# A decoder layer on one core: the set-up of its expert feed-forward stage in another order

## The chip, the cores and the metric

The kernel runs on one core of one Trainium2 chip. The core has five engines that run side by side and meet at semaphores: PE (TensorE, matrix products), ACT (ScalarE), DVE (VectorE), POOL (GpSimd) and SP (SyncE), which here issues all DMAs. The metric is the time of one execution in microseconds (us), lower is better.

## What is computed

One decoder layer over 16 batches of 100 tokens with 128 features: self-attention, cross-attention of 16 heads against a context of 1444 rows, and a feed-forward part with 1024 experts chosen by product keys, each followed by a layer norm. The change touches the third part. Cut to what matters:

```
q = einsum('bnd,de->bne', x, w_q)                    # 2048 = 2 * 8 heads * 128
mean, var = q.mean((0, 1)), q.var((0, 1))            # over all 1600 tokens
q = (q - mean) * rsqrt(var + 1e-5) * bn_gamma + bn_beta
sim = einsum('pbnhd,hkpd->pbnhk', q, keys)           # 32 keys for each of 16 (side, head)
sx, ix = top_k(sim[0], 8); sy, iy = top_k(sim[1], 8)
scores, pk = top_k(all 64 sums of sx and sy, 8)      # -> 8 experts per head
h = gelu_new(x . down_embed[indices]) * softmax(scores)
out = sum of h * up_embed[indices]
x = layernorm(x + out)
```

The kernel never makes q. With cov the 128x128 covariance of the tokens, the variance of column e of q is w_e' cov w_e. So it makes cov, then the 16 variances' groups, scales the keys with gamma / sqrt(var), and folds w_q and the keys into one 128x512 matrix `sim_w`. The similarities of a token are (x - mean) times `sim_w`, plus a constant row `sim_c` = beta times keys.

## The kernel before

`decoder` runs three functions one after the other: `front` (self-attention), `cross`, `ffn`. At the end of each all engines meet, so no engine begins `ffn` before the last batch's `x2` is done. `x2` ([100, 16, 128], tokens of a batch on the partitions) is the output of `cross` and the input of `ffn`. Inside a function each engine has its own list of instructions, written out by hand in the order in which it runs them; an engine waits where its next instruction waits, and everything behind it in the list waits too.

**cross.** 16 batches of 13 tiles (slots 0 to 12 of a batch; 208 tiles). POOL's list goes slot by slot: low halves of the probabilities in slots 0, 3, 4 and 7 (L811), low halves of the queries (`q_lo`, L800), the power for the context's norm in slot 8 (`crs`, L565), the norm itself in slots 9 to 11 (`xh`, L576), and more. A batch's `x2` is finished by DVE (L965) in slot 5 of the next batch.

**ffn, set-up.** SP issues eight loads (L1170), all on one semaphore: `f_wq` (1 MB), `f_wqt` (w_q transposed, two halves of 0.5 MB), `f_keys` (0.25 MB), `f_gam`, `f_bet` (8 KB each), `f_down`, `f_up` (0.5 MB each). PE turns the 16 batches of `x2` (L1500, four groups of four batches) and ACT copies them to `x2T`, adding up each row as it goes (L1219); DVE makes the mean from these sums (L1299, L1301) and centres the four groups into `xcT` (L1305). PE then waits for all eight loads, makes the constant row (16 small products, L1504), turns `xcT` back (L1512; ACT copies to `xct`, L1226), and makes the covariance (16 products over the batches, L1517; ACT: `cov`, L1228). Next the 16 products of `f_wq` with `cov` (L1521), four to a PSUM bank. DVE multiplies each bank by `f_wqt` (L1319) and sums (L1322), corrects the 16 variances twice (L1325, L1327), POOL takes the power -1/2 (`vrs`, L1189), DVE makes `gain` and `kscaled` (L1329, L1331), PE folds (16 products of `f_wqt` with `kscaled`, L1526), ACT copies to `sim_w` (L1238).

Beside this run two other chains. The constant row is split into three bf16 parts: ACT takes the high part (L1223), DVE the rests (`c_rest`, `c_part`, L1308 to L1314), ACT writes them into `sim_c` (L1235, L1236). And three tables of numbers for the one-hot comparisons, `iota_w` (128x128x128), `iota_c` and `iota_j`, are spread out by ACT (L1230 to L1232).

**ffn, steps.** Seven steps of 256 tokens (two halves `hf` of 128; the last has 64 tokens). A step: similarities (PE, L1537 and L1538), their copy `simb` (ACT, L1245), on DVE the 8 largest of each of 32 rows of keys (L1383) and their indices (L1394), then the best pairs, the softmax, and the one-hot tables `oneh`, `eqc`, `mv_hi`, `mv_lo` (L1471 to L1481). From these PE gathers the weights of the experts, 512 products of 16 columns a step (L1560, L1561). PE also makes the experts' hidden values (L1546) and ACT their gelu (L1252). ACT's `idxw` (L1259) and the exponential `esc` (L1283) are needed by DVE in the middle of the step; gelu and exponential need different activation tables, so ACT loads a table before each (ACT_TABLE_LOAD). Gathering of a step runs beside DVE's work of the next.

Of the kernel before, what the change touches and what calls it, by code (L numbers as in the profile page):

```python
# [9 lines left out]
ALU = mybir.AluOpType  # L10
# [3 lines left out]
P = 128  # L14
# [669 lines left out]
def cross(nc, a, m, ps):  # L684
# [6 lines left out]
    with ExitStack() as ctx:  # L691
# [28 lines left out]
        pad_done, cur_done = sem("pad_done"), sem("cur_done")  # L720
# [65 lines left out]
        def _(pool):  # L786
# [32 lines left out]
            current(0)  # L819
            for k in range(P_BUF):  # L820
# [250 lines left out]
def ffn(nc, a, m, ps, out):  # L1071
# [4 lines left out]
    with ExitStack() as ctx, ExitStack() as early:  # L1076
# [6 lines left out]
        ident, nhalf, x2 = m["ident"], m["nhalf"], m["x2"]  # L1083
# [37 lines left out]
        xct = sb("xct", [S, B, D], until=early)  # L1121
        msum, mean = sb("msum", [D, NG], until=early), sb("mean", [D, 1], until=early)
# [8 lines left out]
        f_ld, f_waited = sem("f_ld"), sem("f_waited")  # L1131
        fc_done, x2T_ps, x2T_done, mean_done, xcT_done = (sem(n) for n in ("fc_done", "x2T_ps", "x2T_done", "mean_done", "xcT_done"))
        xct_ps, xct_done, cov_ps, cov_done = (sem(n) for n in ("xct_ps", "xct_done", "cov_ps", "cov_done"))
        cw_ps, cw_done, var_done, vrs_done, gain_done = (sem(n) for n in ("cw_ps", "cw_done", "var_done", "vrs_done", "gain_done"))
        simc_ps, simc_hi, simc_rest, simc_done = (sem(n) for n in ("simc_ps", "simc_hi", "simc_rest", "simc_done"))
        simw_ps, simw_done, wide_done = sem("simw_ps"), sem("simw_done"), sem("wide_done")
# [7 lines left out]
        block = ctx.enter_context(nc.Block())  # L1144

# [15 lines left out]
        def _(sp):  # L1161
            for dst, src in ((f_wq[:, :], a["L0_ffn_w_q"]),
                             (f_wqt[:, 0:FH, :], a["ffn_wq_t"][0:FH * KD, :].rearrange("(n e) d -> e n d", e=KD)),
                             (f_wqt[:, FH:NB, :], a["ffn_wq_t"][FH * KD:NB * KD, :].rearrange("(n e) d -> e n d", e=KD)),
                             (f_keys[:, :, :], a["ffn_keys_t"].rearrange("e s h k -> e (s h) k")),
                             (f_gam[:, :], a["L0_ffn_bn_gamma"]),
                             (f_bet[:, :], a["L0_ffn_bn_beta"]),
                             (f_down[:, :], a["ffn_down_t"]),
                             (f_up[:, :, :], a["L0_ffn_up_embed"].rearrange("(c e) d -> e c d", e=P))):
                sp.dma_start(dst, src).then_inc(f_ld, 16)  # L1170
# [8 lines left out]
        def _(pool):  # L1179
            pool.iota(iota_i[:, :], pattern=[[1, P]], base=0, channel_multiplier=0).then_inc(fc_done, 1)  # L1180
# [7 lines left out]
            pool.wait_ge(var_done, 3)  # L1188
            pool.tensor_tensor(out=vrs[:, :], in0=var[:, :], in1=nhalf[:, 0:NB], op=ALU.pow).then_inc(vrs_done, 1)  # L1189
# [26 lines left out]
        def _(act):  # L1216
            for k in range(NG):
                act.wait_ge(x2T_ps, k + 1)
                act.activation(x2T[:, k * G * S:(k + 1) * G * S], ps[:, k, 0:G * S], ACT.Copy,  # L1219
                               accum_out=msum[:, k:k + 1]).then_inc(x2T_done, 1)  # L1220
            act.wait_ge(fc_done, 6)
            act.wait_ge(simc_ps, 1)
            act.activation(sim_c[0:1, :], ps[0:1, 6, :], ACT.Copy).then_inc(simc_hi, 1)  # L1223
            for k in range(NG):
                act.wait_ge(xct_ps, k + 1)
# [441 lines left out]
```

## Time and profile before

| | |
|---|---|
| time, median of 3 runs | 1341.62 us (1341.55 to 1344.81) |
| profiled execution | 1341.98 us, of which the span 1340.2 us |
| PE busy | 1156.0 us, 86% |
| DVE busy | 1152.7 us, 86% |
| ACT busy | 876.6 us, 65% |
| POOL busy | 620.2 us, 46% |

The span goes from the first to the last instruction of the profile. Busy shares are means over stages that differ: `cross` takes some 910 us, the set-up of `ffn` some 45 us, its steps some 267 us. PEclk in the rows below is the clock granted to TensorE as a share of its full speed; it has two levels, 0.50 (1.2 GHz) and 1.00 (2.4 GHz), and a value between them is a mean over a stretch that holds both.

### The profile page before, as it was taken

The numbers are of one execution on the slowest core, as the hardware profiler recorded it, in microseconds if no ns is written. First come the engines' busy times: TensorE is split into PE (matmuls) and PEld (weight loads), VectorE is DVE, ScalarE is ACT, GpSimd is POOL, SyncE is SP. The second block draws the span as 40 slices with busy tenths as digits, with TensorE's granted clock in tenths as the row PEclk, the third lists the DMA queues.
The fourth block names the chain that finished last, engine by engine and source line by source line (L and its number), as shares of the span: only waits on it lengthen the run. The fifth ranks groups of instructions, "written<-read, shape, count | busy, mean of one in ns | idle before, by whom it ended". The sixth has DMA issues, their size and how long they took to land. (4 is left out here: it accounts for less than half of the span.)

```text
span 1340.2 us, 32623 instructions
## 1 busy us (share of the span) xinstructions
PE 1156.0 (86%) x12753; PEld 900.3 (67%) x12758; DVE 1152.7 (86%) x2860; ACT 876.6 (65%) x1202; POOL 620.2 (46%) x512
## 2 busy tenths in 40 slices
PE   3576999999999999999999999999995639777778
PEld 2463677777777767776777777777674628677668
DVE  5796899999999999999999999998884288999984
ACT  0246888889888888888888888888872632222121
POOL 2344667566675667757577575775220000000000
PEclk9768999999999999999999999999997766666666
DMA  7007999999999999999999999999997000000000
GB/s 156 1 6 139 191 191 187 203 200 190 200 192 201 193 194 196 199 198 198 193 200 198 195 199 193 184 184 173 189 193 162 11 0 2 5 5 6 5 5 6
DMA packets 671121, 185.78 MB, mean 139 GB/s; under 512 B 655828, under 2 KB 668536, under 8 KB 670840
## 3 DMA queue, kind: packets, MB, share of 16 engines
q1 hardware_dynamic: 670968, 183.71, 80.3%
q8 instruction: 100, 1.64, 0.5%
q14 instruction: 53, 0.43, 0.1%
HBM read 19.51 MB, written 0.82 MB: 15 GB/s over the span
## 5 line engine op out<-in xcount | busy, mean ns | idle before, releaser
L1046 PE MATMUL ps<-pT,xa_hi 128*128 128x128 f16 x2288 | 381.1, 217 | 17.5 <-DMA pT<-p 16.7
L851 ACT ACTIVATE e<-ps,bias 128x1444 f32<-128x1444 f32 (+1 forms) x208 | 305.7, 1470 | 132.6 <-DVE bias L923 132.0
L1042 PE MATMUL ps<-pT,xa_hi 128*128 128x128 f16 x2288 | 382.8, 217 | 8.5 <-ACT uT L874 8.2
L1043 PE MATMUL ps<-pT,xa_lo 128*128 128x128 f16 x2288 | 382.8, 217 | 0.0
L921 DVE TENSOR_REDUCE nmax<-ps 128x1 f32<-128x1444 f32 (+1 forms) x208 | 343.9, 1653 | 19.3 <-PE ps L1026 18.6
L933 DVE TENSOR_TENSOR p<-e,p 128x1408 f16<-128x1408 f32 (+3 forms) x288 | 303.9, 1096 | 35.6 <-ACT p L859 34.5
L859 ACT ACTIVATE p<-e 128x1408 f16<-128x1408 f32 (+1 forms) x208 | 288.2, 1386 | 13.3
L811 POOL TENSOR_TENSOR p<-e,p 128x1408 f16<-128x1408 f32 (+1 forms) x128 | 196.6, 1556 | 182.9 <-ACT p L859 182.9
L1042 PEld LDWEIGHTS ps<-pT,xa_hi 128*128 128x128 f16 x2288 | 222.1, 98 | 33.6 <-issue 19.1
L1046 PEld LDWEIGHTS ps<-pT,xa_hi 128*128 128x128 f16 x2288 | 222.0, 98 | 24.2 <-DMA pT<-p 24.0
L1024 PE MATMUL ps<-xT_hi,q_hi 128*128 128x512 f16 (+1 forms) x624 | 229.9, 368 | 8.0 <-DMA xT_lo<-xa_lo 7.4
L1043 PEld LDWEIGHTS ps<-pT,xa_lo 128*128 128x128 f16 x2288 | 222.0, 98 | 13.7
L1025 PE MATMUL ps<-xT_hi,q_lo 128*128 128x512 f16 (+1 forms) x624 | 229.7, 368 | 0.0
L1026 PE MATMUL ps<-xT_lo,q_hi 128*128 128x512 f16 (+1 forms) x624 | 229.7, 368 | 0.0
L576 POOL TENSOR_SCALAR xh<-raw,cmv,crs 128x127 f32<-128x127 f32 x168 | 185.7, 1116 | 0.0
L800 POOL TENSOR_TENSOR q_lo<-q,q_hi 128x400 f16<-128x400 f32 x64 | 89.4, 1397 | 151.9 <-ACT q_hi L893 151.9
L1560 PE MATMUL ps<-mv_hi,oneh 128*128 128x16 f16 (+1 forms) x832 | 109.2, 214 | 46.0 <-DVE mv_lo L1481 46.0
L1560 PEld LDWEIGHTS ps<-mv_hi,oneh 128*128 128x128 f16 (+1 forms) x832 | 108.7, 174 | 48.9 <-DVE mv_lo L1481 48.4
L1197 POOL TENSOR_TENSOR comb<-top 128x512 f32<-128x512 f32 (+1 forms) x13 | 13.7, 1070 | 220.1 <-DVE top L1383 220.1
L1561 PEld LDWEIGHTS ps<-mv_lo,oneh 128*128 128x128 f16 (+1 forms) x832 | 108.5, 174 | 0.9 <-issue 0.8
L1561 PE MATMUL ps<-mv_lo,oneh 128*128 128x16 f16 (+1 forms) x832 | 109.0, 214 | 0.0
L1026 PEld LDWEIGHTS ps<-xT_lo,q_hi 128*128 128x128 f16 x624 | 61.2, 98 | 66.6 <-issue 1.5
(225 smaller groups left out, 1910.4 us busy)
## 6 DMA issues: line engine op xcount, KB each, us to landing
raw<-in_ctx SPq DMA_DIRECT2D x16, 704.0 KB
pT<-p SPq DMA_TRANSPOSE x416, 4.2
f_wq<-in_L_ffn_w_q SPq DMA_DIRECT2D x1, 1024.0 KB, 4.9
f_wqt<-in_ffn_wq_t SPq DMA_DIRECT2D x2, 512.0 KB, 7.0
raw<-in_ctx SPq DMA_DIRECT2D x48, 18.0 KB
x_tok<-in_x SPq DMA_DIRECT2D x1, 800.0 KB
out_x<-ost SPq DMA_DIRECT2D x6, 128.0 KB, 2.0
wk_t<-in_wk_t SPq DMA_DIRECT2D x1, 512.0 KB, 5.7
```

Source lines behind the costliest of these rows:

```text
L851: act.activation(e32[t % E_BUF][rows, :], score_banks(t)[rows, 0:T], ACT.Exp, bias=bias[rows, t % N_BUF:t % N_BUF + 1]).then_inc(e_done, 1)
L859: act.activation(p[t % P_BUF][rows, 0:TF * P], e32[t % E_BUF][rows, 0:TF * P], ACT.Copy).then_inc(hi_done, 1)
L921: dve.tensor_reduce(nmax[rows, k:k + 1], score_banks(t)[rows, 0:T], AX_X, ALU.max, negate=True).then_inc(max_done, 1)
L933: ins = dve.tensor_tensor(out=p[t % P_BUF][rows, out:out + keys.stop - keys.start], in0=e32[t % E_BUF][rows, keys], in1=p[t % P_BUF][rows, ...
L1024: pe.matmul(out, hi, xT_hi[b % 2][:, keys], start=True, stop=False)
L1025: pe.matmul(out, lo, xT_hi[b % 2][:, keys], start=False, stop=False)
L1026: last = pe.matmul(out, hi, xT_lo[b % 2][:, keys], start=False, stop=True)
L1042: pe.matmul(out, hi, ph, start=n == 0, stop=False)
L1043: pe.matmul(out, lo, ph, start=False, stop=False)
L1046: pe.matmul(out, hi, pl, start=False, stop=False)
L1560: pe.matmul(dst, oneh[0:j, :, s], mv_hi[0:j, 0:nb, s], start=True, stop=False)
L1561: last = pe.matmul(dst, oneh[0:j, :, s], mv_lo[0:j, 0:nb, s], start=False, stop=True)
```

## The change

1. **Mean.** POOL adds up `x2` over the batches during `cross` (new tile `x2sum`, one add in slot 7 of each batch). In `ffn` DVE adds the last batch (`total`), and PE multiplies by a tile of ones: the mean's sum stands once as a row on all partitions and once as a column.
2. **Centring in place.** DVE subtracts the mean from `x2` with its tokens on the partitions (`xc`), four groups; the covariance is made from `xc`. The turns back of `xcT` and the copies `xct` are gone, and so are ACT's row sums.
3. **Order of the turned copies.** Of `x2T` and `xcT` only the first group of 400 tokens is made before the covariance. The other three come after the similarities of step 0 (PE, ACT) and after the indices of step 0 (DVE).
4. **Halves.** Variance corrections (two instructions joined into one), power, `gain`, `kscaled`, folding, `sim_w` and the similarities of step 0 are done for 8 of the 16 (side, head) pairs at a time. Step 0's similarities go to four half-filled banks, and DVE takes its maxima half by half.
5. **Loads.** Order `f_wq`, `f_bet`, `f_gam`, `f_keys`, `f_wqt` (two), `f_down`, `f_up`, with four semaphores instead of one, each waited for where it is used.
6. **Constant's rests** on DVE: behind the first half of the keys, ahead of the last variance sum. The constant row on PE: behind the weight products.
7. **Tables.** `iota_w` in four quarters: POOL one in the set-up, ACT one behind `cov`, ACT one ahead of the first gelu, POOL one behind the first `comb`. `iota_c` and `iota_j` on POOL.

The core of the diff:

```diff
@@ cross, POOL
+                if i == 7 and 0 < b < B:
+                    pool.wait_ge(y_norm, 4 * b)
+                    pool.wait_ge(x2sum_done, b)
+                    pool.tensor_tensor(out=m["x2sum"][:, :], in0=m["x2sum"][:, :], in1=x2[:, b - 1, :], op=ALU.add).then_inc(x2sum_done, 1)
@@ ffn, POOL
             pool.tensor_copy(iota_f[:, :], iota_i[:, :]).then_inc(fc_done, 1)
-            pool.wait_ge(var_done, 3)
-            pool.tensor_tensor(out=vrs[:, :], in0=var[:, :], in1=nhalf[:, 0:NB], op=ALU.pow).then_inc(vrs_done, 1)
+            wide_rows(0)
+            for p in range(2):
+                pool.wait_ge(var_done, p + 1)
+                pool.tensor_tensor(out=vrs[:, key_half(p)], in0=var[:, key_half(p)], in1=nhalf[:, 0:FH], op=ALU.pow).then_inc(vrs_done, 1)
...
             for i in range(NSTEP):
                 combine(i)
+                if i == 0:
+                    wide_rows(1)
@@ ffn, ACT
+            turned_out(0)
+            act.wait_ge(cov_ps, 1)
+            act.activation(cov[:, :], ps[:, 0, 0:D], ACT.Copy, scale=1.0 / NT).then_inc(cov_done, 1)
...
+            weights_out(0)
...
+            first_out(0)
+            weights_out(1)
+            first_out(1)
+            for k in range(1, NG):
+                turned_out(k)
+            wide_rows(3)
@@ ffn, DVE
+            dve.tensor_tensor(out=total[:, :], in0=x2sum[:, :], in1=x2[:, B - 1, :], op=ALU.add).then_inc(total_done, 1)
+            dve.wait_ge(mean_ps, 1)
+            for k in range(NG):
+                ks = slice(k * G, (k + 1) * G)
+                dve.scalar_tensor_tensor(out=xc[:, ks, :], in0=ps[0:S, 3, 0:D].rearrange("s (a d) -> s a d", a=1).to_broadcast([S, G, D]),
+                                         scalar=-1.0 / NT, in1=x2[:, ks, :], op0=ALU.mult, op1=ALU.add).then_inc(xc_done, 1)
...
+                if i == 0:
+                    for k in range(1, NG):
+                        centred(k)
+                    dve.wait_ge(narrow_done, 1)
@@ ffn, PE
+            pe.matmul(ps[0:S, 3, 0:D], ones_s[:, :], total[:, :], start=True, stop=True)
+            pe.matmul(ps[:, 3, D:D + 1], total[:, :], ones_s[:, 0:1], start=True, stop=True).then_inc(mean_ps, 1)
+            turn(0)
+            for b in range(B):
+                if b % G == 0:
+                    pe.wait_ge(xc_done, b // G + 1)
+                last = pe.matmul(ps[:, 0, 0:D], xc[:, b, :], xc[:, b, :], start=b == 0, stop=b == B - 1)
+            last.then_inc(cov_ps, 1)
...
+            sim_weights(0)
+            pe.wait_ge(simc_done, 1)
+            pe.wait_ge(xcT_done, 1)
+            first_sims(0)
+            sim_weights(1)
+            first_sims(1)
+            for k in range(1, NG):
+                turn(k)
```

PE's list from its start in `ffn` (`ps` is PSUM; `ident` stands for a turn). Before:

```order
L1500 MATMUL ps<-ident,x 128x100 x16
L1504 MATMUL ps<-f_keys,f_bet 1x32 x16
L1512 MATMUL ps<-ident,xcT 100x128 x16
L1517 MATMUL ps<-xct 128x128 x16
L1521 MATMUL ps<-cov,f_wq 128x128 x16
L1526 MATMUL ps<-kscaled,f_wqt 128x32 x16
L1537 MATMUL ps<-sim_c,ones_b 128x512
```

And now, up to the other three groups' turns:

```order
L1605 MATMUL ps<-total,ones_s 100x128
L1606 MATMUL ps<-ones_s,total 128x1
L1587 MATMUL ps<-ident,x 128x100 x4
L1611 MATMUL ps<-xc 128x128 x16
L1617 MATMUL ps<-cov,f_wq 128x128 x16
L1622 MATMUL ps<-f_keys,f_bet 1x32 x16
L1593 MATMUL ps<-kscaled,f_wqt 128x32 x8
L1599 MATMUL ps<-sim_c,ones_b 128x256
L1600 MATMUL ps<-sim_w,xcT 128x256
L1599 MATMUL ps<-sim_c,ones_b 128x256
L1600 MATMUL ps<-sim_w,xcT 128x256
L1593 MATMUL ps<-kscaled,f_wqt 128x32 x8
```

The covariance (L1611) has moved ahead of everything that a load is needed for, the constant row (L1622) behind the weight products (L1617), the folding and the first similarities come in two halves.

DVE's list between the weight products and the first maxima. Before:

```order
L1319 TENSOR_TENSOR cw<-ps,f_wqt 128x512
L1322 TENSOR_REDUCE var<-cw 128x4
L1319 TENSOR_TENSOR cw<-ps,f_wqt 128x512
L1322 TENSOR_REDUCE var<-cw 128x4
L1325 TENSOR_SCALAR var<-var 128x16
L1327 TENSOR_SCALAR var<-var 128x16
L1329 TENSOR_TENSOR gain<-vrs,f_gam 128x16
L1331 TENSOR_TENSOR kscaled<-f_keys,gain 128x512
```

And now:

```order
L1362 TENSOR_TENSOR cw<-ps,f_wqt 128x512
L1368 TENSOR_REDUCE var<-cw 128x4
L1362 TENSOR_TENSOR cw<-ps,f_wqt 128x512
L1378 TENSOR_TENSOR gain<-vrs,f_gam 128x8
L1380 TENSOR_TENSOR kscaled<-f_keys,gain 128x256
L1393 TENSOR_TENSOR c_rest<-ps,sim_c 1x512
L1395 CAST c_part<-c_rest 1x512
L1397 TENSOR_TENSOR c_rest<-c_rest,c_part 1x512
L1399 CAST c_part<-c_rest 1x512
L1368 TENSOR_REDUCE var<-cw 128x4
L1372 TENSOR_SCALAR var<-var 128x8
L1378 TENSOR_TENSOR gain<-vrs,f_gam 128x8
```

The keys' first half is scaled ahead of the last variance sum, and the four instructions of the constant's rests stand between the two halves.

ACT's list from the copy of `sim_w` to `esc` of step 0. Before:

```order
L1238 ACTIVATE sim_w<-ps 128x512
L1245 ACTIVATE simb<-ps 128x1024
L1252 ACT_TABLE_LOAD
L1252 ACTIVATE gel<-ps 128x1024 x2
L1259 ACTIVATE idxw<-idxf 128x2048
L1283 ACT_TABLE_LOAD
L1283 ACTIVATE esc<-dsc 128x128
```

And now:

```order
L1275 ACTIVATE sim_w<-ps 128x256
L1279 ACTIVATE sim_c<-c_part 1x512
L1280 ACTIVATE sim_c<-c_part 1x512
L1270 ACTIVATE simb<-ps 128x2x256
L1275 ACTIVATE sim_w<-ps 128x256
L1270 ACTIVATE simb<-ps 128x2x256
L1254 ACTIVATE x2T<-ps 128x400 x3
L1261 ACTIVATE iota_w<-iota_f 128x4096
L1299 ACT_TABLE_LOAD
L1299 ACTIVATE gel<-ps 128x1024 x2
L1306 ACTIVATE idxw<-idxf 128x2048
L1329 ACT_TABLE_LOAD
```

Three turned groups and a quarter of `iota_w` have come between the similarities' copy and the first gelu, with `idxw` and `esc` behind them.

## Rows read from the trace of the kernel before

**Rows 1.** Busy times by stage: us, busy by engine (instructions), PEclk, DMA.

```profile
100.00:1010.00 910.00, 865.97 (x10070) 646.52 (x10071) 829.98 (x1492) 761.87 (x1019) 562.03 (x435) 0.99 1.14 192
1028.00:1073.00 45.00, 26.64 (x168) 23.23 (x169) 10.38 (x22) 23.35 (x21) 4.20 (x7) 0.66 0.26 76
...
1108.00:1340.00 232.00, 188.61 (x2027) 170.53 (x2031) 197.16 (x990) 49.42 (x70) 16.32 (x18) 0.65 0.02 5
```

**Rows 2.** Chain of waits, set-up: start us, us, what, count of records.

```profile
1034.47 6.08 DMA f_up<-in_L_ffn_up_embed
...
1045.73 3.59 PE ps L1517 x32
...
1049.67 1.17 PE ps L1521 x8
...
1056.74 2.94 POOL vrs L1189
...
1060.65 7.05 PE ps L1526 x32
...
1068.85 1.91 PE ps L1538 x2
...
1072.77 1.03 ACT simb L1245
...
1073.92 3.08 DVE top L1383 x32
```

**Rows 3.** Busy times in three stretches with PE at work: PEclk is what counts.

```profile
1040.60:1045.00 4.40, 4.40 (x44) 3.83 (x44) 1.76 (x3) 1.78 (x3) 0.00 (x0) 0.50 0.00 0
1045.20:1053.50 8.30, 7.93 (x69) 7.56 (x68) 2.83 (x5) 5.24 (x4) 0.00 (x0) 1.00 0.01 2
1060.70:1067.70 7.00, 6.99 (x32) 6.85 (x32) 0.00 (x0) 5.86 (x5) 0.00 (x0) 0.50 0.00 0
```

**Rows 4.** Lines in the set-up: engine, shapes, count, busy us, mean ns, idle before.

```profile
L1230 ACT ACTIVATE iota_w<-iota_f 128x16384 f16<-128x16384 f32 x1 | 13.8, 13847 | 0.0
...
L1305 DVE TENSOR_SCALAR xcT<-x2T,mean 128x400 f32<-128x400 f32 x4 | 1.4, 424 | 0.0
...
L1308 DVE TENSOR_TENSOR c_rest<-ps,sim_c 1x512 f32<-1x512 f32 x1 | 0.7, 678 | 9.6 <-ACT sim_c L1223 9.6
```

**Rows 5.** The page's DMA issues: size of each, median us to landing.

```profile
f_wqt<-in_ffn_wq_t SPq DMA_DIRECT2D x2, 512.0 KB, 7.0
```

**Rows 6.** POOL by line over the whole span.

```profile
L576 POOL TENSOR_SCALAR xh<-raw,cmv,crs 128x127 f32<-128x127 f32 x154 | 174.5, 1143 | 0.0
...
L565 POOL TENSOR_TENSOR crs<-cve,nhalf 128x12 f32<-128x12 f32 x16 | 36.4, 2275 | 0.1
...
L791 POOL COPY sc_cur<-sc 128x16 f32<-128x16 f32 x16 | 3.1, 192 | 5.5 <-POOLq L40 5.5
...
L1187 POOL CAST iota_f<-iota_i 128x128 f32<-128x128 int32 x1 | 0.3, 291 | 0.1
```

**Rows 7.** Chain of waits in step 0, as rows 2.

```profile
1077.14 5.26 DVE idx L1394 x33
...
1088.73 0.29 DVE pijf L1428
...
1095.69 8.69 DVE oneh L1471
```

**Rows 8.** Timeline, step 0, ACT: start us, us, engine, instruction [idle before].

```profile
1082.74 1.91 ACT L1259 ACTIVATE idxw<-idxf 128x2048 f16<-128x2048 f16 x1 [3.51 <-DVE idxf L1401]
1084.67 1.28 ACT L1283 ACT_TABLE_LOAD   x1
1085.96 0.31 ACT L1283 ACTIVATE esc<-dsc 128x128 f32<-128x128 f32 x1
```

**Rows 9.** Timeline of PE in the same stretch.

```profile
1095.13 3.62 PE L1546 MATMUL ps<-x2T,f_down 128*128 128x256 f32 x8
```

**Rows 10.** Timeline of POOL behind `crs`, slot 9 of a late batch.

```profile
892.09 1.81 POOL L800 TENSOR_TENSOR q_lo<-q,q_hi 128x400 f16<-128x400 f32 x1 [3.82 <-ACT q_hi L893]
```

More of the change, by code:

```diff
@@ L819, in _ @@
             current(0)
+            pool.memset(m["x2sum"][:, :], 0.0).then_inc(x2sum_done, 1)
             for k in range(P_BUF):
@@ L1144, in ffn, with sim_half, key_half, group @@
         block = ctx.enter_context(nc.Block())
+        HALF_SIM = NB * KEYS // 2
+        def sim_half(p):
+            return slice(p * HALF_SIM, (p + 1) * HALF_SIM)
+        def key_half(p):
+            return slice(p * FH, (p + 1) * FH)
+        def group(k):
+            return slice(k * G * S, (k + 1) * G * S)
         def cols(i):
@@ new lines, in centred, with weighted_cov @@
+            def centred(k):
+                dve.wait_ge(x2T_done, k + 1)
+                dve.tensor_scalar(xcT[:, group(k)], x2T[:, group(k)], mean[:, 0:1], None, ALU.subtract).then_inc(xcT_done, 1)
+            def weighted_cov(k):
+                ns = slice(4 * k, 4 * k + 4)
+                dve.wait_ge(cw_ps, k + 1)
+                if k == 0:
+                    dve.wait_ge(wqt_ld, 32)
+                dve.tensor_tensor(out=cw[:, ns, :], in0=ps[:, k, :].rearrange("e (n d) -> e n d", n=4),
+                                  in1=f_wqt[:, ns, :], op=ALU.mult).then_inc(cw_done, 1)
@@ new lines, in variance, with safe_variance, scaled_keys @@
+            def variance(k):
+                ns = slice(4 * k, 4 * k + 4)
+                dve.wait_ge(cw_done, k + 1)
+                dve.tensor_reduce(var[:, ns], cw[:, ns, :], AX_X, ALU.add).then_inc(sum_done, 1)
+            def safe_variance(p):
+                dve.wait_ge(sum_done, 2 * p + 2)
+                dve.tensor_scalar(var[:, key_half(p)], var[:, key_half(p)], 0.0, EPS, ALU.max, ALU.add).then_inc(var_done, 1)
+            def scaled_keys(p):
+                ns = key_half(p)
+                dve.wait_ge(vrs_done, p + 1)
+                dve.wait_ge(keys_ld, 48)
+                dve.tensor_tensor(out=gain[:, ns], in0=vrs[:, ns], in1=f_gam[:, ns], op=ALU.mult).then_inc(gain_done, 1)
+                dve.wait_ge(gain_done, p + 1)
+                dve.tensor_tensor(out=kscaled[:, ns, :], in0=f_keys[:, ns, :],
+                                  in1=gain[:, ns].rearrange("e (n a) -> e n a", a=1).to_broadcast([KD, FH, KEYS]), op=ALU.mult).then_inc(kscaled_done, 1)
@@ L1307, in _ @@
+            centred(0)
+            for k in range(2):
+                weighted_cov(k)
+                variance(k)
+            safe_variance(0)
+            weighted_cov(2)
+            variance(2)
+            weighted_cov(3)
+            scaled_keys(0)
             dve.wait_ge(simc_hi, 1)
@@ L1314, in _ @@
             dve.tensor_copy(c_part[:, 1, :], c_rest[:, 1, :]).then_inc(simc_rest, 1)
[L1316 to L1333 removed]
+            variance(3)
+            safe_variance(1)
+            scaled_keys(1)
             def weigh(i, n):
@@ L1375, in step @@
                 j, na, nb = nh * HK, nh * NB, nh * NC
-                dve.wait_ge(sim_done, i + 1)
                 if i:
+                    dve.wait_ge(sim_done, i)
                     dve.wait_ge(comb_done, i)
                     dve.wait_ge(pick, 7 * i)
-                dve.sem_inc(f_waited, 1)
+                    dve.sem_inc(f_waited, 1)
+                else:
+                    for p in range(2):
+                        dve.wait_ge(first_done, p + 1)
+                        dve.sem_inc(f_waited, 1)
+                        for hf in range(nh):
+                            for n in range(p * FH, (p + 1) * FH):
+                                ins = dve.max(top[0:w, hf, n, :], simb[0:w, hf, n, :])
+                    ins.then_inc(top_done, 1)
                 for hf in range(nh):
-                    for n in range(NB):
-                        ins = dve.max(top[0:w, hf, n, :], simb[0:w, hf, n, :])
-                    if hf == nh - 1:
+                    if i:
+                        for n in range(NB):
+                            ins = dve.max(top[0:w, hf, n, :], simb[0:w, hf, n, :])
+                    if i and hf == nh - 1:
                         ins.then_inc(top_done, 1)
```

177 lines of the change are left out of this document (85 added, 92 removed).

## The prediction

> **What bounds the kernel now.** I read the stretches by stage first [rows 1]. From 100 to 1010 us PE and DVE are both busy over 90% of the time: that is the cross-attention stage, into which the change puts one short POOL instruction per batch. The set-up of the feed-forward stage (1028 to 1073 us) is different: in 45 us PE is busy 26.6, ACT 23.4 and DVE 10.4 us, so no engine is the bound; it is a chain, one engine working while the others wait. So what counts there is the chain of waits [rows 2]: the last load lands at 1040.55, then turns, 16 covariance products to 1049.3, its copy, four pieces of the variance, POOL's power, the 16 products that fold keys into weights (7.05 us), the first similarities, their copy, and 32 maxima until 1077.0. From there to the first `oneh` at 1095.69 step 0 is DVE's own chain, with hardly a gap [rows 7]. From 1095.69 on the code is the same in both kernels, so the gain is how much earlier `oneh` of step 0 starts, plus or minus what TensorE's clock does to the later steps.
>
> **The sum, from 1028.1 us.** Set-up loads no longer stand ahead of the covariance. New order: DVE adds `x2sum` and the last batch (0.3), PE makes the mean by two fp32 products of full weights (0.44 each at half clock, as 7.05 us for 16 in [rows 2]), so the mean stands at 1029.4. The first `xc` group reads 512 columns from PSUM, as `c_rest` does in 0.68 [rows 4]: 1030.1. Later groups take 0.65 each, less than PE's four products. The 16 covariance products cost 0.22 each at full clock (3.59 us for 16 in [rows 2]) and 0.44 at half. Before, PE took up work at 1040.6, stood at clock 0.50 up to 1045.0 and at 1.00 from 1045.2 [rows 3]. I let it rise as late here, 4.5 us into the products: ten at 0.44 and six at 0.22, done at 1036.1, copied at 1036.4. Before that copy was done at 1049.65 (start of its reader, 1049.67, in [rows 2]). **Saved: 13.2**, with ends 15.5 (all at full clock) and 12.1 (all at half).
>
> The products with the queries' weights then need `f_wqt` too. Its halves landed 7.0 us after issue behind 2 MB [rows 5]; now 0.25 MB of keys and the two small loads go ahead, an eighth more bytes, so 7.9 us: about 1036.9. The first four products are done at 1036.4 + 1.2 = 1037.6, so this load is hidden by only 0.7 us.
>
> DVE runs product, sum, product, sum at 0.7 each (512 columns, as `c_rest` in [rows 4]) and one short correction: 1040.6. POOL's power over 16 columns took 2.94 [rows 2], over 12 it took 2.28 [rows 6], so 0.165 a column and 1.6 for 8: 1042.3. DVE meanwhile does three more pieces (to 1042.6), then gain and half of the keys: 1043.2. PE folds eight keys (1.8 at full, 3.5 at half clock), ACT copies 0.4: 1045.5 to 1047.2. Beside it DVE makes the constant's rests (two of 0.68, two casts of 0.4): 1045.4; ACT writes them, two of 0.6: 1046.8. I take 1046.8, since the rests decide unless the clock has fallen already.
>
> From here the clock matters. All that PE has after 1040.5 are products of 32 columns. Such a run stood at 0.50 for 7.0 us while PE was busy 6.99 of them [rows 3], though 7.9 busy us out of 8.3 had been at 1.00 shortly before. So I take half clock from 1046.8. First similarities at half width: 512 columns took 1.91 [rows 2], so 0.95 for 256 and 0.15 for the bf16 constant, two tokens' halves: 2.2, to 1049.0; ACT 0.6. The second half's scaled keys are ready by 1048.7 (sum 0.7, correction 0.2, POOL 1.7, DVE 0.6 from 1045.4), so PE goes on: eight folds 3.5, ACT 0.4, products 2.2, ACT 0.6: 1055.9. DVE has done half the maxima by 1051.3; the other 16 take 1.54 (3.08 for 32): **maxima done at 1057.5 instead of 1077.0, 19.5 earlier.**
>
> **What comes back.** Two things stand in step 0 that did not. DVE centres the other three groups ahead of `idxf`: four took 1.44 us, so **1.1** for three [rows 4]. And ACT, which before had 3.51 us of idle ahead of `idxw` [rows 8], gets late. From 1055.9 it takes three turned groups (0.8 on PE and 0.5 on ACT each, one PSUM bank for all three, so in turns): 1059.7. Then a quarter of `iota_w`: 13.85/4 = 3.5 [rows 4], 1063.2. Then the table load 1.28 and the first `gel`, 128x1024 from PSUM like `simb`'s 1.03 [rows 2]: 1065.5. PE's second eight `f_down` records take 3.62 at half clock [rows 9]: 1069.2; `gel` 1070.3; `idxw` 1.91: 1072.2; load and `esc` 1.6: 1073.8. DVE gets through 32 indices (5.3, [rows 7]), the three centred groups and `idxf` at 1064.3, and 6.3 us later (1082.71 to 1089.02, [rows 7]) wants `esc`, at 1070.6. It **waits 3.3** (1.6 if PE is at full clock there). Sum: 19.5 - 1.1 - 3.3 = **15.1 us**.
>
> Of the table load the rows show this: it ends at 1085.95 and `esc` starts at 1085.96 [rows 8]. The Trainium skill, page "ScalarE: Activation LUTs", section "What ACT_TABLE_LOAD costs", says that a drain of about 1.38 us comes on top of each load of 1.28. By that rule ACT would be 2.8 us later and the kernel would take 1329.3 us; the row shows no such drain, so that has a chance of 2 in 100.
>
> **Edits costed at nothing.** POOL's new add per batch (100x128) stands behind `low_half` of slot 7 and ahead of `crs`; behind it in the queue are `crs` and `q_lo`. By POOL's rate for two inputs it takes some 0.4 us. POOL then sits idle 3.82 us until `q_hi` comes [rows 10]: covered. Without that cover, 15 times 0.4 is 6 us. Its wait is for the layer norm of the batch before, done many slots earlier. POOL's table pieces: a cast of 128 elements takes 0.29, a power over one column more costs 0.165 [rows 6]; the copy of 16 columns takes 0.19, so 0.86 ns an element: `iota_c`, `iota_j` and a quarter of `iota_w` (6208 elements) are done by 1035.5, and POOL is wanted at 1040.6. At the worst rate that a cast allows (0.29 for 128, 2.27 ns) they end at 1044.3, 3.7 late. ACT's first quarter fits between 1036.4 and the constant at 1042. POOL's second quarter starts at 1059.7 and is wanted at 1080.6.
>
> **Rivals.** (1) The clock holds. If PE stays at 1.00 after 1045, folds take 1.8 and products 1.2: second copy at 1053.0, maxima at 1054.5 (22.5 earlier), ACT late by only 1.3; 20.1 us saved, **1321.5**. For it: once up, it held through 8.3 us [rows 3]. Against: the narrow products above. 20 in 100. (2) The clock rises late, or a load or POOL is. With all products at half clock the copy is at 1037.5, the 16 weight products end at 1044.6, the constant row at 1046.5, its rests are written at 1050.6 instead of 1046.8: 3.8 lost, 11.3 saved, **1330.3**. `f_wqt` 3 us late or POOL at 2.27 ns give about the same. For it: only 0.7 us of cover on the load, and PE idles before 1028. 20 in 100. (3) The gain is given back in later steps: they run at a mean clock of 0.65, PE 188.6 of 232 us [rows 1], and the stretches at full clock may fall elsewhere. The three runs already lie 3.3 us apart. To take back 11 us or more PE would have to lose 6% of its time there with DVE never covering: 3 in 100, about **1339**. (4) Slower: POOL's pieces ahead of the power. The one-input `xh` instruction costs 1.14 us for 127 elements, 9 ns each [rows 6]. At that rate 6208 elements end at 1086, 45 us after the variance, and the second quarter 16 us after `oneh` wants it: 61 - 15 = 46 us slower, **1388**. It decides from 4.9 ns an element on. Against: `xh` has two per-partition operands, the cast row has none. 2 in 100.
>
> **Numbers.** The profiled run took 1341.98 us (span 1340.2), 0.36 above the median of 1341.62. 1341.62 - 15.1 = 1326.5. The forecast holds 53 in 100, beside the 2 of the drain. Rivals 1 and 2 give 1321.5 and 1330.3; with some 2 us either way for the later steps' clock the range is 1319.5 to 1332.5. A measurement tells 0.3%, 4 us, from no change: faster 0.95, same 0.03, slower 0.02.
>
> **What the profile after should show.** The copy of `cov` ends 8.3 us after the stage starts (21.6 before); PE's first fp32 products of 32 columns start at once behind the weight products, with no wait for DMA; maxima of step 0 done 29.4 us in (48.9 before); DVE waits some 3 us for `esc` in step 0; `oneh` starts 52.5 us in (67.6 before). The forecast is wrong if PE waits for `f_wqt` or `f_wq`, if POOL still copies when the variance is ready, if the clock in the second half of the set-up is 1.00, or if the stretch from `oneh` to the end is not 244.5 us within 3.

## The result and the profile after

| | before | after |
|---|---|---|
| time, median | 1342.78 us (1341.55 to 1344.81, 4 runs) | 1325.98 us (1325.4 to 1329.02, 4 runs) |
| ratio, with its 95% interval | | 0.9878 (0.9857 to 0.9899) |
| profiled execution, its span | 1341.98, 1340.2 us | 1325.4, 1323.7 us |

The changed kernel is 16.8 us faster by the medians. The forecast was 1326.5 with a range from 1319.5 to 1332.5. Six further runs in a group of their own gave the same ratio, 0.9878 (`c_after` below).

The page of the changed kernel, its totals and its row of granted clock:

```profile
span 1323.7 us, 32659 instructions
PE 1155.8 (87%) x12752; PEld 901.2 (68%) x12752; DVE 1159.2 (88%) x2866; ACT 865.3 (65%) x1195; POOL 636.4 (48%) x534
PEclk9768999999999999999999999999999776666666
```

PE kept its work and DVE gained 6.5 us. ACT's work fell by 11.3 us and POOL's rose by 16.2, the tables and, on POOL, 6.9 us of adds; neither engine is near full. What went is idle time in the set-up. The chain of waits of the changed kernel, of the stretch that [rows 2] and [rows 7] show of the kernel before (start, length, engine and line; the first SP load was issued at 1026.91, which is the zero of all times given as "in"):

```profile
1026.96 0.30 DVE total L1344
...
1029.11 6.79 PE ps L1611 x32
...
1035.93 0.29 ACT cov L1258
...
1036.26 1.17 PE ps L1617 x8
...
1037.45 0.70 DVE cw L1362
...
1042.89 1.99 PE ps L1593 x16
...
1044.90 0.38 ACT sim_w L1275
...
1045.31 0.63 ACT sim_c L1279
...
1048.94 3.27 PE ps L1593 x16
...
1058.51 3.50 ACT iota_w L1261
...
1064.41 3.79 PE ps L1652 x8
...
1069.14 1.90 ACT idxw L1306
...
1071.06 1.28 ACT L1329
...
1072.36 0.32 ACT esc L1329
...
1079.46 8.69 DVE oneh L1556
```

In [rows 2] a load, turns, the covariance, the whole variance and one run of 16 folds stood one behind the other. Here DVE begins 0.05 us into the stage, and no load is in the chain. From `cov` to 1048.94 PE, DVE and ACT hand over a half at a time. Then, from 1055 on, the chain runs along ACT: its quarter of `iota_w`, `gel`, `idxw`, table load, `esc`. That is the part of the gain that comes back. DVE's row where it meets that chain, with its idle time in brackets:

```profile
1072.70 0.29 DVE L1513 TENSOR_REDUCE ssum<-esc 128x16 f32<-128x128 f32 x1 [2.22 <-ACT esc L1329]
```

The same point of the program, counted from the first load of the stage (for the kernel before, 1028.11):

| us in | before | forecast | after |
|---|---|---|---|
| `cov` copied | 21.5 | 8.3 | 9.30 |
| maxima of step 0 done | 48.9 | 29.4 | 30.45 |
| DVE waits for `esc` | 0 | 3.3 | 2.22 |
| `oneh` of step 0 starts | 67.6 | 52.5 | 52.55 |
| from there to the end | 244.5 | 244.5 | 244.24 |

So 15.0 us of the span's 16.5 are in the set-up. Another 0.3 lies behind it and 1.2 us ahead of it, in a cross-attention stage whose only new instruction is POOL's add.

### The profile page after: what moved, and what is told of

Same layout as the page of the kernel before. It is cut to its first block and busy times, and to the rows that moved or that the text cites. A ratio compares the mean times of both kernels' runs of the same rounds, so it can differ in the third digit from the quotient of the medians.

```text
span 1323.7 us, 32659 instructions
## 1 busy us (share of the span) xinstructions
PE 1155.8 (87%) x12752; PEld 901.2 (68%) x12752; DVE 1159.2 (88%) x2866; ACT 865.3 (65%) x1195; POOL 636.4 (48%) x534
## 5 line engine op out<-in xcount | busy, mean ns | idle before, releaser
L938 DVE TENSOR_TENSOR p<-e,p 128x1408 f16<-128x1408 f32 (+3 forms) x288 | 304.3, 1097 | 33.5 <-ACT p L864 32.2
```

The lines of the kernel that those rows point to most:

```text
L938: ins = dve.tensor_tensor(out=p[t % P_BUF][rows, out:out + keys.stop - keys.start], in0=e32[t % E_BUF][rows, keys], in1=p[t % P_BUF][rows, ...
```

## The experiments

Each kernel ran on one chip together with runs of the kernel before. "Set-up" is from the first load's issue to the start of `oneh` of step 0, from the profiled execution: 67.58 us before, 52.55 after. It says more of a change in the set-up than the whole time does, since the stage itself began anywhere from 1026.9 to 1032.1 us in the fourteen profiled executions of these kernels, and the stretch behind `oneh` took 241.8 to 245.1 us. Each set-up is read from one execution. Where the code up to `oneh` does the same, it came out within 0.1 us (52.55, 52.45 in c_after, 52.46 in e7) or 0.6 us (67.58, 68.22 in e3); where the covariance met another clock it moved more. The whole times of e5, e6, e7, e8 and e10 can't be told from the changed kernel's, so what is said of their parts rests on the profiled execution.

| kernel | time, us (runs) | ratio to before, 95% | set-up | maxima done, us in |
|---|---|---|---|---|
| before, beside three groups of these kernels | 1344.22 (18), 1343.29 (7), 1344.64 (11) | 1 | 67.58 | 48.9 |
| e1_loads | 1338.26 (6) | 0.9954 (0.9937 to 0.9971) | 61.79 | 43.1 |
| e2_one_load | 1334.08 (5) | 0.9924 (0.9904 to 0.9943) | 56.95 | 34.9 |
| e3_x2sum | 1344.71 (12) | 1.0003 (0.9988 to 1.0018) | 68.22 | 49.5 |
| e4_tables_on_act | 1334.61 (5) | 0.9920 (0.9902 to 0.9938) | 60.74 | 39.9 |
| e8_in_sequence | 1327.90 (4) | 0.9881 (0.9864 to 0.9897) | 53.99 | 32.0 |
| e5_quarter_late | 1325.03 (4) | 0.9871 (0.9850 to 0.9892) | 50.97 | 30.0 |
| e6_fill | 1327.36 (4) | 0.9884 (0.9868 to 0.9901) | 49.42 | 27.5 |
| e7_prewarm | 1327.96 (4) | 0.9884 (0.9865 to 0.9904) | 52.46 | 30.4 |
| c_after | 1328.42 (6) | 0.9878 (0.9854 to 0.9901) | 52.45 | 30.4 |
| e9_late_fill | 1321.91 (6) | 0.9829 (0.9805 to 0.9854) | 46.77 | 27.0 |
| e10_late_fill_warm | 1327.34 (6) | 0.9864 (0.9838 to 0.9890) | 48.97 | 29.2 |
| e11_pool_quarter | 1329.86 (1) | one run only | 55.58 | 33.5 |

### Which parts carry the gain

**e1_loads**: the kernel before with the new order of loads alone, four semaphores, and a wait at each first use.

```diff
+            sp.dma_start(f_wq[:, :], ...).then_inc(wq_ld, 16)
+            ... f_bet, f_gam, f_keys ... .then_inc(keys_ld, 16)
+            ... f_wqt, two halves ... .then_inc(wqt_ld, 16)
+            ... f_down, f_up ... .then_inc(expert_ld, 16)
-            pe.wait_ge(f_ld, 16 * 8)
+            pe.wait_ge(keys_ld, 48)
```

> The kernel before with only the loads changed: the new order (f_wq, f_bet, f_gam, f_keys, f_wqt twice, f_down, f_up), four semaphores, and PE's constant row waits for the keys alone. Theory of the prediction: all of the set-up before hung on the last load at 12.4 us after the stage began; the keys land some 6.2 us in, so the chain starts 6 us earlier and the kernel takes 6 us less, 1336.7 us. That is less than half of what the whole change gave, the rest being the covariance ahead of the loads and the halves. Rival: the loads are the whole gain and the rest only moves waits about; then it is 14 us or more faster, below 1329.

Set-up 61.79, 5.8 us less. PE's timeline of this kernel shows what still holds it (the columns are start, length, instruction, and in brackets the idle time before it with its releaser; the row ends with the window, after 23 of its 32 records):

```profile
1033.84 1.39 PE L1508 MATMUL ps<-f_keys,f_bet 128*1 128x32 f32 x23 [3.19 <-DMA f_keys<-in_ffn_keys_t]
```

The constant row still stands ahead of the covariance and waits for the keys, 6.1 us in; before, it waited for all eight loads until 12.4 us in. The load order alone is worth 5.8 us.

**e2_one_load**: the changed kernel with the old load order on one semaphore.

```diff
-            pe.wait_ge(wq_ld, 16)
+            pe.wait_ge(wq_ld, 16 * 8)
...
-                    dve.wait_ge(wqt_ld, 32)
+                    dve.wait_ge(wq_ld, 16 * 8)
```

> The changed kernel with the old order of loads on one semaphore, which PE waits for ahead of the weight products. Theory: the weight products start 9.3 us into the stage and the last load lands at 12.4, so everything behind shifts by 3.1 us: 1329 us. Rival (the order of loads carries the gain): it loses 6 us or more, 1332 or above. Rival (loads are now hidden altogether): no loss, 1326.

PE in this kernel (the first row ends with its window, after 5 of 32 records), and the clock of two stretches of it (columns: stretch, its length, busy time and instructions of PE, PEld, DVE, ACT, POOL, granted clock, share and rate of the DMAs):

```profile
1042.96 1.41 PE L1616 MATMUL ps<-cov,f_wq 128*128 128x128 f32 x5 [4.49 <-DMA f_up<-in_L_ffn_up_embed]
...
1038.50:1042.90 4.40, 0.00 (x0) 0.00 (x0) 0.00 (x0) 3.89 (x2) 0.00 (x0) 0.70 0.91 271
1043.00:1045.00 2.00, 2.00 (x9) 2.00 (x10) 0.00 (x0) 0.00 (x0) 0.00 (x0) 0.50 0.00 0
```

PE waits 4.49 us and the clock falls in the wait, so the weight products take 5.76 us instead of 3.84. The set-up grew by 4.4, where 3.1 was expected: the missing 1.3 is the price of the clock, which I had left out. Undoing the load order costs less (4.4) than doing it alone gave (5.8), since in the rebuilt set-up 8.3 us of work precede the first wait for a load.

**e4_tables_on_act**: the changed kernel with all three tables on ACT behind `cov`, as it stood before.

```diff
             act.activation(cov[:, :], ps[:, 0, 0:D], ...)
-            wide_rows(2)
+            act.activation(iota_w[:, :, :], ..., ACT.Copy)
+            act.activation(iota_c[:, :, :], ..., ACT.Copy)
+            act.activation(iota_j[:, :, :], ..., ACT.Copy).then_inc(narrow_done, 1)
```

> The changed kernel with all three tables on ACT behind the copy of cov, as before the change. Theory: ACT is busy 16 us there (13.85 + 1.9 + 0.24) and the high part of the constant, sim_w and simb stand behind it in its list: maxima of step 0 some 10 us later, of which the wait for esc (2.2) is given back: 7 us slower than the changed kernel, 1333. Rival: tables were hidden before and stay hidden; no loss, 1326.

The chain of this kernel:

```profile
1041.04 0.28 ACT cov L1248
1041.34 13.86 ACT iota_w L1250
1055.20 1.80 ACT iota_c L1251
1056.99 0.14 ACT iota_j L1252
1057.14 0.49 ACT sim_c L1255
```

The tables cost nothing before, since the variance, the power and the folds took as long beside them ([rows 2] has no `iota_w`). In the shorter set-up they would have been the chain: +8.2 us (by the ratios of the whole times, 0.9920 against 0.9878, it is 5.6). By these rows, distributing them (part 7) would bring nothing by itself, though that was not run. It keeps the rest from being lost.

**e8_in_sequence**: the changed kernel with both halves taken one step at a time (all four variance sums, both powers with the constant's rests beside them, then both folds, then all similarities).

```diff
-            for k in range(2):
+            for k in range(4):
                 weighted_cov(k)
                 variance(k)
             safe_variance(0)
-            weighted_cov(2)
-            variance(2)
-            weighted_cov(3)
-            scaled_keys(0)
+            safe_variance(1)
             ...
-            variance(3)
-            safe_variance(1)
+            scaled_keys(0)
             scaled_keys(1)
             ...
             sim_weights(0)
+            sim_weights(1)
             ...
             first_sims(0)
-            sim_weights(1)
             first_sims(1)
```

> The changed kernel with its halves one behind the other instead of interleaved: all four variance pieces, both corrections, the rests, both scalings; both folds ahead of the similarities. Theory: the overlap of the halves is worth 2.5 us at the maxima of step 0; oneh at 55 instead of 52.55. Rival: the halves buy nothing since PE is the bound from the folds on: 52.5.

Set-up 53.99, 1.4 us more and not 2.5. But its covariance met an earlier rise of the clock, `cov` copied 8.18 us in and not 9.30. From there to the maxima it took 23.8 us, the changed kernel 21.15, which makes the overlap of halves worth 2.65 us. But the early clock enters this comparison, since an earlier `cov` meets `f_wqt`:

```profile
1041.58 0.69 DVE L1362 TENSOR_TENSOR cw<-ps,f_wqt 128x512 f32<-128x512 f32 x1 [2.52 <-DMA f_wqt<-in_ffn_wq_t]
```

DVE's first product starts 1.78 us behind `cov` here and 1.24 behind it in the changed kernel. The better match is e5 below, which up to the maxima is the changed kernel and had `cov` 8.08 us in: its maxima are done at 29.99 and e8's at 31.98. So the overlap is worth 2.0 to 2.65 us.

**e3_x2sum**: the kernel before with POOL's 15 adds alone.

```diff
+                if i == 7 and 0 < b < B:
+                    pool.wait_ge(y_norm, 4 * b)
+                    pool.wait_ge(x2sum_done, b)
+                    pool.tensor_tensor(out=m["x2sum"][:, :], in0=m["x2sum"][:, :], in1=x2[:, b - 1, :], op=ALU.add)...
```

> The kernel before with POOL's adds of x2 in slot 7 of each batch, whose sum nobody reads. Theory: POOL's 3.8 us of idle behind each covers 15 adds of some 0.4 us; no change, 1342.8 within 1.5. Rival: the adds push q_lo or the low halves and cost their own time, 15 times 0.4, 6 us: 1349.

POOL's groups from 100 to 1000 us in that kernel:

```profile
L800 POOL TENSOR_TENSOR q_lo<-q,q_hi 128x400 f16<-128x400 f32 x64 | 89.0, 1391 | 147.0 <-ACT q_hi L898 147.0
...
L840 POOL TENSOR_TENSOR x2sum<-x2sum,x 100x128 f32<-100x128 f32 x15 | 6.9, 458 | 0.0
```

An add takes 0.46 us, `q_lo` still sits idle for 147 us in sum waiting for `q_hi`, and the time is 1.0003 (0.9988 to 1.0018) of before: covered, as costed.

### What stands in the gain's way: ACT's late quarter and the clock

**c_after** is the changed kernel again, on the chip of e9 to e11.

> The changed kernel itself, as the comparison for the others of this call. From the stage's start to oneh 52.5 us or, where TensorE's clock comes up earlier in the covariance, 51 us; after oneh 244 us; whole time 1326 within 2, most of what moves being where the cross-attention ends.

It repeats set-up 52.45, maxima 30.35 us in, a wait of 2.22 us for `esc`.

**e5_quarter_late**: ACT's second quarter of `iota_w` behind `esc` and the next similarities' copy, no longer ahead of the first `gel`.

```diff
                 turned_out(k)
-            wide_rows(3)
...
                 if i + 1 < NSTEP:
                     sims_out(i + 1)
+                if i == 0:
+                    wide_rows(3)
```

> The changed kernel with ACT's second quarter of iota_w behind esc and the second similarities' copy of step 0, where ACT is idle 5.6 us, instead of ahead of the first gelu. Theory: DVE's wait for esc in step 0 (2.22 us) is made of ACT's queue, and 3.6 us of it are this quarter; the wait goes, and the stretch from the stage's start to oneh falls from 52.55 to 50.3 us, the kernel by 2.2. Rival: idxw or PE's hidden values decide, and nothing changes: 52.5.

Set-up 50.97. The wait for `esc` shrank from 2.22 to 1.09 us. It did not go, because PE's `f_down` products ran at half clock in both their batches (3.66 and 3.78 us); the second:

```profile
1064.68 3.78 PE L1653 MATMUL ps<-x2T,f_down 128*128 128x256 f32 x8 [1.11 <-ACT gel L1298]
```

0.5 of the 1.6 us that the set-up lost is an earlier clock in the covariance (maxima at 29.99), so the move itself is worth 1.1. The half of it that is missing sits in the clock.

**e6_fill**: 14 idle products of 128 columns into an unused bank, whose result nobody reads. Seven stand behind the constant row, seven behind the first folds.

```diff
+            def filler(n):
+                for _ in range(n):
+                    pe.matmul(ps[:, 7, 0:D], f_wq[:, 0:KD], cov[:, :], start=True, stop=True)
+            pe.wait_ge(x2T_done, 1)
+            filler(7)
             sim_weights(0)
+            filler(7)
             pe.wait_ge(simc_done, 1)
```

> The changed kernel with 14 products more on PE, whose results nobody reads (128 columns each, fp32, weights and cov as in the weight products): seven behind the constant row, seven behind the first eight folds, in stretches where PE has nothing. Theory: TensorE's clock fell to 0.50 some 18.6 us into the stage because PE had only products of 32 columns and gaps; with wide products there it stays at 1.00, the second folds take 2.0 instead of 3.3 and the four similarities' products 0.6 instead of 1.05 each: maxima of step 0 done 3 us earlier, oneh at 48 to 49.5 us instead of 52.55. Rival: the clock falls anyway, 52.5, or the fillers hold up the chain, 53 or more.

The stretch from the second folds on, first in the changed kernel and then in e6_fill (clock is the third number from the end):

```profile
1045.80:1052.00 6.20, 5.37 (x22) 4.83 (x22) 2.22 (x19) 1.36 (x3) 1.64 (x1) 0.50 0.00 0
```

```profile
1044.60:1048.40 3.80, 3.80 (x34) 3.61 (x33) 3.64 (x8) 0.73 (x2) 0.30 (x1) 1.00 0.00 0
1048.50:1054.70 6.20, 5.22 (x37) 4.14 (x37) 2.27 (x19) 1.79 (x4) 1.64 (x1) 1.00 0.00 0
```

The fillers fill PE's idle time ahead of the first folds and ahead of the first similarities, the clock stays at 1.00, and the second folds take 1.97 us where they took 3.46. Maxima are done at 27.49 instead of 30.45. Filler and gap go together here: whether the width of the fillers or the filled idle time kept the clock up was not tested. The result confirms rival 1's price for the clock: it had 3.0 us between the two cases at the maxima (1057.5 and 1054.5), and 2.96 were measured. The whole time did not move measurably from the changed kernel's (0.9884 against 0.9878): DVE still waited 2.03 us for `esc`, and the set-up's 3.1 us are less than what the stage's start and the later steps scatter by.

**e9_late_fill**: e5 and e6 together.

> The changed kernel with two edits: ACT's second quarter of iota_w behind esc, and 14 idle wide products on PE. Theory: the quarter alone left 1.1 us of the wait for esc since the second hidden values ran at half clock (3.8 us) behind a gap on PE; with the fillers the clock is up and the gap short, so they take 2.0 and the wait is gone. oneh 47.3 us after the stage's start (49.4 with the fillers alone), the kernel some 5 us below the changed one, 1321. Rival: the gap still brings the clock down, 48.5.

Set-up 46.77, 5.7 us under c_after, and 1321.91 us (1319.56 to 1325.55) against 1328.42 (1326.64 to 1330.96) on the same chip; the two sets of runs do not overlap. ACT and PE in step 0 of this kernel:

```profile
1063.11 1.99 PE L1660 MATMUL ps<-x2T,f_down 128*128 128x256 f32 x8 [1.11 <-ACT gel L1298]
```

```profile
1067.98 1.28 ACT L1328 ACT_TABLE_LOAD   x1
1069.27 0.31 ACT L1328 ACTIVATE esc<-dsc 128x128 f32<-128x128 f32 x1
...
1070.39 3.61 ACT L1261 ACTIVATE iota_w<-iota_f 128x4096 f16<-128x4096 f32 x1
```

The second `f_down` batch runs at full clock, `esc` is there before DVE (`ssum` at 1070.71) asks, and the quarter is done before `oneh` at 1077.46. Of the 5.7 us, 0.7 came with an earlier `cov` (copied 8.53 us in, 9.21 in c_after). The other 5.0 are more than the two edits gave apart (1.1 and 3.1), since each had left a part of the wait for `esc` standing. It is the fastest kernel of the study.

**e7_prewarm**: seven products of the last cross-attention kind, result unused, at the end of `cross`.

```diff
+            pe.wait_ge(e_done, ALL_TILES)
+            for _ in range(7):
+                pe.matmul(ps[0:S, 0, 0:D + 1], uT[:, 0:S], w2h[:, 0, :], start=True, stop=True)
```

> The changed kernel with seven products more on PE at the end of the cross-attention (129 columns, fp32, into a bank that is free), in its last 3.2 us of idle before the feed-forward stage. Theory: the covariance ran at 0.50 (6.8 us) because PE had been idle before it; the clock comes up earlier and the covariance takes 4 to 5.5 us. f_wqt, which lands some 8.5 us in, then becomes the bound, so oneh comes 1 to 2 us earlier: 50.5 to 51.5. Rival: the covariance stays at half clock, 52.5.

No gain, set-up 52.46. The clock of its stretches: the seven products, the stage's first 1.7 us, the covariance, the weight products:

```profile
1027.35:1029.05 1.70, 1.70 (x16) 1.49 (x14) 1.15 (x5) 0.00 (x0) 0.03 (x1) 1.00 0.00 0
1029.50:1031.20 1.70, 0.48 (x5) 0.51 (x6) 0.64 (x2) 0.00 (x0) 1.03 (x6) 1.00 0.00 0
1032.06:1038.80 6.74, 6.74 (x32) 6.59 (x32) 5.58 (x5) 0.24 (x1) 5.40 (x3) 0.54 1.03 323
1039.20:1043.00 3.80, 3.79 (x33) 3.67 (x34) 2.23 (x4) 3.60 (x1) 0.00 (x0) 1.00 0.88 265
```

The clock was up when the seven products ran and still up 1.0 us into the stage; it was down when the covariance began. The theory that they would carry it through the covariance fell.

**e10_late_fill_warm**: e9 with 13 such products at the end of `cross`, where e7 had seven.

> As the kernel with the late quarter and the fillers, and 13 products on PE at the end of the cross-attention instead of the seven that did not do. Seven ran at full clock in 1.7 us and the clock still fell before the covariance; 13 take 3.1 us and fill the gap. Theory: the covariance runs at 1.00, 3.8 instead of 6.8 us, and f_wqt becomes the bound, so oneh comes 1.5 us earlier than without: 45.8 us. Rival: the clock falls as before and the fillers only delay: 47.5 or more.

Now the covariance ran at 1.00 in 3.84 us and `cov` was copied 5.97 us in, 2.6 earlier than in e9. This was not a longer copy of e7: the clock was already at 0.50 when the 13 products began, they took 4.23 us, and it rose while they ran (1.00 in the last of them). They ended at 1030.95, behind DVE's last instruction of `cross` (1029.37), and DVE waited 1.88 us for the new stage where it waits 0.33 in e7 and e9. So they also held up the stage by 1.55 us, which the set-up, counted from the stage's first load, does not contain. And the set-up was 48.97, longer than e9's 46.77. DVE in this kernel, and the clock of PE's stretches ahead of and in the first folds:

```profile
1041.58 0.69 DVE L1366 TENSOR_TENSOR cw<-ps,f_wqt 128x512 f32<-128x512 f32 x1 [2.92 <-DMA f_wqt<-in_ffn_wq_t]
```

```profile
1044.20:1046.90 2.70, 0.00 (x0) 0.00 (x0) 2.60 (x8) 0.00 (x0) 1.67 (x1) 0.88 0.02 6
1047.00:1050.50 3.50, 3.49 (x17) 3.49 (x17) 2.81 (x6) 0.00 (x0) 0.47 (x1) 0.50 0.00 0
```

`f_wqt` is what the earlier covariance meets: its halves landed 7.3 us after issue (median of the two), so DVE's first product could begin 10.37 us in, where in e9 it had begun 9.77 in. The fillers, placed for the later time, were used up, PE stood idle 3.1 us ahead of the folds, and the clock fell to 0.50 before them (3.62 us instead of 1.97). The first product's 0.6 us and the folds' 1.65 make up the 2.2 us against e9. The whole time is 5.4 us above e9's; what these 2.2 and the 1.55 leave of it is within the scatter of the stage's start and the later steps. My expectation had the covariance and the load right and the sum wrong: 45.8 left out the idle time that a late load opens ahead of the folds, and the clock with it. With the loads as they are, nothing ahead of `cov` is worth shortening by more than about a microsecond: where the load released DVE's first product, it started 9.49 to 10.46 us in (e5, e7, e8, e10), in the changed kernel 10.54.

### DVE behind a cast of POOL

In the changed kernel DVE's first centred group took 3.40 us, where the same instruction takes 0.42 elsewhere. DVE and POOL there:

```profile
1030.95 3.40 DVE L1355 TENSOR_SCALAR xcT<-x2T,mean 128x400 f32<-128x400 f32 x1
```

```profile
1030.53 3.60 POOL L1217 CAST iota_w<-iota_f 128x4096 f16<-128x4096 f32 x1
```

It ends at 1034.35, 0.22 us after POOL's cast (1034.13). Nothing waited for it, since DVE's next instruction, at 1037.45, waited for PE.

**e11_pool_quarter**: POOL's first quarter of `iota_w` behind both powers.

```diff
-            wide_rows(0)
             for p in range(2):
                 pool.wait_ge(var_done, p + 1)
                 pool.tensor_tensor(out=vrs[:, key_half(p)], ..., op=ALU.pow).then_inc(vrs_done, 1)
+            wide_rows(0)
```

> The changed kernel with POOL's first quarter of iota_w behind the second power instead of ahead of the first. In the changed kernel DVE's first centred group of 400 columns took 3.40 us beside that cast, against 0.42 for each group in the kernel before. Theory: DVE's instruction waits until POOL's cast has ended, since both need one way into SBUF; without the cast beside it, it takes 0.42 us. The time stays, since DVE waits for the weight products anyway: oneh at 52.5 us. Rival: it is slow for another reason (its source, its place) and stays at 3.4.

The centred group took 0.43 us again, as that theory said. But the set-up, in this one run, grew by 3.0 us, where I had expected none. POOL and DVE behind the second power:

```profile
1048.51 3.60 POOL L1217 CAST iota_w<-iota_f 128x4096 f16<-128x4096 f32 x1
```

```profile
1048.59 3.53 DVE L1378 TENSOR_TENSOR gain<-vrs,f_gam 128x8 f32<-128x8 f32 x1 [1.76 <-POOL vrs L1221]
```

`gain` over 8 columns takes 0.16 us; here it ends 0.01 us after the cast. So the block moved with the cast, from a place where DVE had time to the middle of the chain. The Trainium skill, page "SBUF — State Buffer", section "SBUF: two separate sides", says that the two engines share a port pair which one instruction holds for its whole length while the other fully blocks, among others when the DVE instruction has two SBUF inputs and POOL's reads SBUF. By that rule, `gain` (two inputs) must wait out the cast, which reads `iota_f`, and the row agrees (3.53 us beside a cast of 3.60). Its other kind, an instruction in a two-port mode, would cover the centred group; no run here shows in which mode that ran.

## Why the prediction was right, point by point

- **The bound** was named rightly: a chain with idle engines, not a busy engine. The kernel's busy times hardly changed (PE 1156.0 to 1155.8, DVE 1152.7 to 1159.2) and the time fell by 16.8 us.
- **`cov` copied at 8.3**: a step mis-sized, 9.30. I let the clock rise 4.5 us into the products: ten at 0.44 and six at 0.22 make 5.7 us, and my points in time leave them 6.0. It rose with the last few only, 6 us into them, and they took 6.79. The other 0.2 is their start, 2.2 us in for 2.0. In other executions the same products took from 5.57 us (e5; 5.66 in e8, 5.79 in e2, 6.01 in e9) to 6.85 (e6), so this term has a spread of 1.3 us that I had put down as a rival's alone. The measured value lies between the forecast and the bound "all at half clock", whose 7.0 us it nearly reached.
- **`f_wqt` hidden by 0.7 us**: it landed 6.6 us after issue by the page of the profile (7.9 forecast), and DVE's first product was released by PE, as forecast. The cover was real and thin: e5, e7, e8 and e10 have this load in their chains, and in e10 it cost 2.9 us of wait.
- **POOL.** The copy rate of 0.86 ns an element held nearly: 1.89 us for 2048 (0.92), 3.60 for 4096 (0.88). All was done by 1034.13, 6.3 us ahead of the variance. The power over 8 columns took 1.67 (1.6 forecast). Rival 4 (9 ns an element) is out. What I had not in the sum is that a POOL cast can stop DVE; it was harmless where it stood.
- **Half clock from the first similarities on.** Forecast 0.50 from 1046.8, 18.7 us in. Measured: it fell between 1045.4 and 1045.6, 18.6 us in, with PE idle since the first folds had ended 0.7 us before. It rose again at 1055.7, which I had not forecast. Rival 1 did not come, and e6 shows that its price was right (2.96 us at the maxima).
- **What comes back: right in sum by luck.** Three centred groups took 1.29 us (1.1 forecast). The wait for `esc` was 2.22, not 3.3. It is the difference of two arrivals. ACT had `esc` done 45.76 us in, where the prediction's points give 45.7. DVE asked for it 43.57 us in, 1.1 later than the 42.5 forecast, nearly all of it the microsecond lost in the covariance. ACT had lost it too (second copy of the similarities done 28.7 us in, 27.8 forecast) and got it back in the three turned groups, 2.9 us instead of 3.8: PE made the first beside that copy, and the other two took 0.56 each at full clock (0.93 at half, in e5). So `oneh` at 52.55 against 52.5 rests on two terms that were each off by about a microsecond with opposite signs, the covariance and the turned groups. The second `f_down` batch ran at half clock as forecast (3.78 us, 3.62 forecast); the first, at full clock, ended 3.6 us ahead of the `gel` that reads it and decided nothing.
- **The table load.** `esc` starts 0.02 us after its 1.28 us load ends (1071.06 to 1072.36), in e9 0.01 us. The drain of the Trainium skill, page "ScalarE: Activation LUTs", section "What ACT_TABLE_LOAD costs", does not appear, as [rows 8] had shown.
- **The later steps** took 244.24 (244.5 within 3): rival 3 is out for this change.
- **1.2 us of the span's gain** lie in cross-attention, where e3 shows that the add does nothing measurable. The stage's start scatters by 5 us over the executions profiled, so I take them as scatter. Whether a part of it belongs to the change is open.

What each part is worth, by the runs: the load order 4.4 to 5.8 us, the overlap of halves 2.0 to 2.65. The remaining 6.5 to 8.6 of the 15.0 us must be the shorter way to `cov` (mean from POOL's sum, no turns back, one group of turns) and the constant row taken out of it, less what comes back; that is the difference and was not run by itself. The tables' move saves 8.2 us which the other parts would otherwise have lost.

## What to carry to other kernels

Where engines hand over to each other in a chain, write the sum as points in time ("so many us in") and not only as durations: the two errors here, which cancel in the total, are seen because each point had a forecast. Work that was free beside a long chain (the tables) becomes the chain when it shrinks, so its move belongs to the same change. And before shortening a stretch further, look what stands a microsecond behind it: in e10 a covariance 2.6 us earlier met a load, used up the fillers before their time and ended 2.2 us slower.

## What the runs showed of the hardware that was not expected

- Idle products of 128 columns between narrow ones kept the granted clock at 1.00 (e6, 10.0 us at 1.00 in the two stretches shown), though not to the end of the set-up everywhere: in e9 the last similarities took 0.91 us and the turned groups behind them 0.93 each, against 0.60 and 0.56 in e6. Without them it stood at 0.50 while PE was busy 5.37 of 6.20 us with products of 32 and 256 columns.
- Seven products at 1.00 that ended 1.67 us ahead of the stage's first product did not carry the clock into the covariance (0.54 over it). 13 that ended 0.74 us ahead did (1.00 over it, 3.84 us instead of 6.79). The 13 began at 0.50 and the clock rose in them, the seven began at 1.00; whether that, their number or the shorter pause made the difference was not tested.
- The clock fell in a wait of PE of 4.49 us (e2) and in one of 3.1 us (e10), which makes a wait dearer than its length: the weight products behind the first took 1.9 us more, the folds behind the second 1.65.
- A POOL cast of 3.60 us held a 0.42 us DVE instruction for 3.40 and a 0.16 us one for 3.53.
